# Four of sixteen key pairs get their row maximum through a difference and a ReLU on ScalarE

## The reference

```
h = layernorm(x) * g + b                       # 4096 x 256
q = h @ Wq, k = h @ Wk, v = h @ Wv             # 16 heads of 16 columns each
scores = q k^T / sqrt(16)                      # per head, 4096 queries x 4096 keys
attn = softmax(scores)                         # needs max over the keys of each query
ctx = attn @ v
```

## Time and profile before

| | us |
|---|---|
| median of 3 runs | 3914.32 (3910.07 to 3921.57) |
| the profiled execution's own time | 3921.57 |
| its span in the profile | 3919.8 |

### The profile page before, as it was taken

One profiled execution on the slowest core, in us unless ns is written; L12 is line 12 of the kernel. 1 busy time (PEld: TensorE's weight loads), 2 busy tenths in 40 slices (PEclk: granted clock), 3 DMA queues, 4 the chain that ended last, 5 costly groups with the idle time before them and its releaser, 6 DMA issues. The chain is left out here.

```text
span 3919.8 us, 86423 instructions
## 1 busy us (share of the span) xinstructions
PE 3547.9 (91%) x29108; PEld 1917.4 (49%) x29108; DVE 3020.9 (77%) x5498; ACT 2509.0 (64%) x2773; POOL 697.2 (18%) x703
## 2 busy tenths in 40 slices
PE   7479999999999999999999999999999806999990
PEld 4244444444444444444444444444444605999980
DVE  1638999999999999999999999999996522333335
ACT  2124777777777777777777777777778103555540
POOL 0000000000000000000000000000000357888856
PEclk8686999999999999999999999999999757999995
DMA  2240010110101101010110101011000623444424
GB/s 95 86 143 16 13 20 13 22 20 13 22 11 21 20 12 22 11 21 14 20 21 13 20 13 20 13 22 20 13 13 6 217 89 125 146 137 138 143 83 133
DMA packets 153010, 196.17 MB, mean 50 GB/s; under 512 B 49041, under 2 KB 118545, under 8 KB 148113
## 3 DMA queue, kind: packets, MB, share of 16 engines
q1 hardware_dynamic: 134240, 163.29, 14.9%
q0 software_dynamic: 6336, 16.79, 1.4%
q10 hardware_dynamic: 12144, 12.06, 0.9%
HBM read 128.30 MB, written 62.65 MB: 49 GB/s over the span
## 5 line engine op out<-in xcount | busy, mean ns | idle before, releaser
L725 DVE TENSOR_REDUCE unit_max<-m_ps 128x1 f32<-128x512 f32 x4096 | 2568.3, 684 | 131.4 <-PE m_ps L622 128.7
L704 ACT ACTIVATE probs<-s_ps 128x1024 f32<-128x1024 f32 x2048 | 2084.4, 1026 | 630.0 <-PE s_ps L630 624.6
L645 PE MATMUL o_ps<-probs,v_here 128*32 128x256 f32 (+1 forms) x15360 | 1283.7, 406 | 0.5 <-ACT probs L704 0.5
L622 PE MATMUL m_ps<-k_ring,q_stage 48*128 48x512 f32 x4096 | 1017.8, 422 | 41.5 <-DVE unit_max L725 22.9
L630 PE MATMUL s_ps<-q_stage,k_ring 50*128 50x512 f32 x4096 | 1024.0, 493 | 0.4 <-ACT probs L704 0.4
L630 PEld LDWEIGHTS s_ps<-q_stage,k_ring 50*128 50x128 f32 x4096 | 385.2, 184 | 818.9 <-issue 646.2
L622 PEld LDWEIGHTS m_ps<-k_ring,q_stage 48*128 48x128 f32 x4096 | 665.7, 188 | 183.6 <-DVE unit_max L725 160.3
L645 PEld LDWEIGHTS o_ps<-probs,v_here 128*32 128x32 f32 x15360 | 303.2, 108 | 507.8 <-issue 504.8
L571 POOL TENSOR_TENSOR neg_max<-no_max,tile_max 128x4 f32<-128x4 f32 x127 | 25.3, 199 | 2480.5 <-DVE tile_max L740 2480.5
L1458 DVE TENSOR_TENSOR hidden_low<-h_ps,hidden_high 128x512 fp32r<-128x512 f32 x184 | 127.4, 692 | 366.4 <-ACT hidden_high L1422 366.4
L1418 ACT ACTIVATE h_ps<-h_ps,b_here 128x512 f32<-128x512 f32 x184 | 121.4, 660 | 255.3 <-PE h_ps L1355 255.3
(11 more groups left out here) (175 smaller groups left out, 1948.3 us busy)
## 6 DMA issues: line engine op xcount, KB each, us to landing
w_in<-in_W SPq DMA_DIRECT2D x46, 1024.0 KB, 4.9
q_stage<-max_turned SPq DMA_DIRECT2D x2048, 0.5 KB
q_stage<-qs_dram SPq DMA_DIRECT2D x768, 32.0 KB, 1.8
k_ring<-ks_dram SPq DMA_DIRECT2D x96, 128.0 KB, 4.2
slots_dram<-zero_rows SPq DMA_DIRECT2D x24, 512.0 KB, 6.7
rows_e<-slots_dram SPq DMA_DIRECT2D x24, 512.0 KB, 3.9
y_slots_dram<-y_out ACTq DMA_DIRECT2D x23, 512.0 KB, 4.3
qs_dram<-parts SPq DMA_DIRECT2D x16, 512.0 KB, 2.8
```

The costliest lines, as they stand in the source:

```text
L622: nc.tensor.matmul(m_ps[:, b % 3, :], q_stage[at:at + SROWS, col:col + P], k_ring[at:at + SROWS, par, key:key + CHUNK], start=True, stop=T ...
L645: last = nc.tensor.matmul(o_ps[at:at + SQ, lo:hi], v_here[:, par, first_tile(t) + 2 * k, :], probs[:, t, k, lo:hi], start=(pair == 0), sto ...
L704: nc.scalar.activation(probs[:, t, :, :], s_ps[:, t % 2, :, :], ACT.Exp).then_inc(exp_done, 1)
L725: nc.vector.tensor_reduce(unit_max[:, b, qt, 2 * j + k:2 * j + k + 1], m_ps[:, block_of(t, k) % 3, :], AX.X, ALU.max).then_inc(m_read, 1 + ...
```

## The change

For every query, max(a, b) = b + max(a - b, 0). The change uses this for a pair of key blocks, a from side 0 and b from side 1, in four of the sixteen units of a chunk (`RELU_PAIRS`: 2, 5, 11, 14).

- Key preparation: DVE writes the difference of the two key sides to `k_diff` (a copy of one half out of PSUM, and a subtraction), ACT rounds it to a fifth high part, DVE computes its low part, and SP stores both with two further DMAs per chunk. `low_ready` and `high_ready` count 5 per chunk and not 4.
- SP loads this difference for each head into `kd_ring`, with three further DMAs per head.
- In the four units PE's k = 0 matmul reads `kd_ring` in place of `k_ring`, which gives q(a - b). ACT takes its ReLU out of the bank into `excess` (SBUF), in front of the unit's exponential. DVE adds the other bank to it and takes the maximum, in one `tensor_tensor_reduce`, in place of two reductions.
- The matmul that follows in the first bank's ring place waits for ACT's `excess_ready`, and no longer for `m_read`.

```diff
+RELU_PAIRS = (2, 5, 11, 14)
 ...
             def split(c, b, more):
                 for s in range(4):
-                    dve.wait_ge(high_ready, c * 4 + (s + 1))
+                    if s == 2:
+                        dve.wait_ge(high_ready, c * 5 + 4)
+                        nc.vector.tensor_scalar(k_diff[:, :, :], qk_ps[:, 2:4, HALF:CHUNK], 1.0, None, ALU.mult
+                                                ).then_inc(half_copied, 1)
+                        dve.wait_ge(half_copied, c + 1)
+                        nc.vector.tensor_tensor(k_diff[:, :, :], qk_ps[:, 2:4, 0:HALF], k_diff[:, :, :],
+                                                ALU.subtract).then_inc(diff_ready, 1)
+                    dve.wait_ge(high_ready, c * 5 + (s + 1))
                     nc.vector.scalar_tensor_tensor(parts[:, b, s, 1, :], qk_ps[:, s, :], DH ** -0.5 if s < 2 else 1.0,
                                                    parts[:, b, s, 0, :].bitcast(F32), ALU.mult, ALU.subtract
                                                    ).then_inc(low_ready, 1)
+                dve.wait_ge(high_ready, c * 5 + 5)
+                nc.vector.tensor_tensor(parts[:, b, 4, 1, :].rearrange("p (j t) -> p j t", j=HALVES), k_diff[:, :, :],
+                                        parts[:, b, 4, 0, :].bitcast(F32).rearrange("p (j t) -> p j t", j=HALVES),
+                                        ALU.subtract).then_inc(low_ready, 1)
 ...
                     b = block_of(t, k)
-                    if c * RING_BLOCKS + b > 2:
+                    past = [r for r in RELU_PAIRS if block_of(r, 0) in (b - 3, b - 3 + RING_BLOCKS)]
+                    if past and c * RING_BLOCKS + b > 2:
+                        done = sum(r < t for r in RELU_PAIRS)
+                        pe.wait_ge(excess_ready, it * (PAIR * len(RELU_PAIRS)) + (c * len(RELU_PAIRS) + done))
+                    elif c * RING_BLOCKS + b > 2:
                         pe.wait_ge(m_read, it * (PAIR * RING_BLOCKS) + (c * RING_BLOCKS + b - 2))
+                    ring = kd_ring if k == 0 and t in RELU_PAIRS else k_ring
 ...
+            def excess_pair(n, t):
+                act.wait_ge(m_done, n * (2 * UNITS) + (2 * t + 1))
+                nc.scalar.activation(excess[:, :], m_ps[:, block_of(t, 0) % 3, :], ACT.Relu).then_inc(excess_ready, 1)
 ...
                 for t in range(UNITS):
+                    if ahead and t in RELU_PAIRS:
+                        excess_pair(i + LEAD, t)
                     act.wait_ge(s_done, i * UNITS + (t + 1))
 ...
+                if t in RELU_PAIRS:
+                    dve.wait_ge(excess_ready, n * len(RELU_PAIRS) + (RELU_PAIRS.index(t) + 1))
+                    dve.wait_ge(m_done, n * (2 * UNITS) + (2 * t + 2))
+                    dve.sem_inc(dve_passed, 1)
+                    nc.vector.tensor_tensor_reduce(excess[:, :], m_ps[:, block_of(t, 1) % 3, :], excess[:, :], 1.0, LEAST,
+                                                   ALU.add, ALU.max, unit_max[:, b, qt, 2 * j:2 * j + 1]
+                                                   ).then_inc(m_read, 2 + skip)
+                    return
```

More of the change, by code:

```diff
@@ L52 @@
 LEAST = -3.4e38
-HEAD_DMAS = 16 * 2 * len(K_PARTS)
+HEAD_DMAS = 16 * 3 * len(K_PARTS)
 Q_DMAS = 16 * 2 * len(Q_PARTS)
@@ L133, in linear_attention @@
         hT = sb("hT", [P, 2, HALVES, CHUNK])
-        parts = sb("parts", [P, 2, 4, PARTS, CHUNK], F32R)
+        k_diff = sb("k_diff", [P, HALVES, HALF])
+        parts = sb("parts", [P, 2, 5, PARTS, CHUNK], F32R)
         banks = ps("banks", [P, 8, CHUNK])
@@ L206, in _ @@
                                          ).then_inc(parts_out[b], 16)
-                    sp.wait_ge(parts_out[b], it * 96 + 96)
+                    sp.wait_ge(low_ready, c * 5 + 10)
+                    for j in range(HALVES):
+                        dst = dram["kd"][:, P * j:P * j + P, ds(c * HALF, HALF)]
+                        sp.dma_start(dst.rearrange("n p t -> p n t"),
+                                     parts[:, b, 4, :, HALF * j:HALF * j + HALF].bitcast(F32)).then_inc(parts_out[b], 16)
+                    sp.wait_ge(parts_out[b], it * 128 + 128)
                     sp.sem_inc(parts_free, 1)
             for b in range(2):
-                sp.wait_ge(parts_out[b], 16 * 6 * CHUNKS // 2)
+                sp.wait_ge(parts_out[b], 16 * 8 * CHUNKS // 2)
             sp.wait_ge(x1_out, 16)
@@ L341, in split @@
                                          scale=(DH ** -0.5 if s < 2 else 1.0)).then_inc(high_ready, 1)
+                act.wait_ge(diff_ready, c + 1)
+                nc.scalar.activation(parts[:, b, 4, 0, :], k_diff[:, :, :], ACT.Copy).then_inc(high_ready, 1)
                 if more:
@@ L487, in load_head @@
                                      dram["ks"][part, ds(h * DH, DH), side, :]).then_inc(head_in, 16)
+                for n, part in enumerate(K_PARTS):
+                    sp.dma_start(kd_ring[DH * n:DH * n + DH, ds(par, 1), :].bitcast(F32).rearrange("r a k -> r (a k)"),
+                                 dram["kd"][part, ds(h * DH, DH), :]).then_inc(head_in, 16)
             def load_q(h, qc, buf):
@@ L619, in max_pair @@
                     b = block_of(t, k)
-                    if c * RING_BLOCKS + b > 2:
+                    past = [r for r in RELU_PAIRS if block_of(r, 0) in (b - 3, b - 3 + RING_BLOCKS)]
[3 more added lines that the diff above has]
+                    elif c * RING_BLOCKS + b > 2:
                         pe.wait_ge(m_read, it * (PAIR * RING_BLOCKS) + (c * RING_BLOCKS + b - 2))
+                    ring = kd_ring if k == 0 and t in RELU_PAIRS else k_ring
                     nc.tensor.matmul(m_ps[:, b % 3, :], q_stage[at:at + SROWS, col:col + P],
-                                     k_ring[at:at + SROWS, par, key:key + CHUNK], start=True, stop=True).then_inc(m_done, 1)
+                                     ring[at:at + SROWS, par, key:key + CHUNK], start=True, stop=True).then_inc(m_done, 1)
             def scores(it, c, t):
@@ L697, in copy_o, with chunk @@
                 nc.scalar.activation(o_here[:, :], o_ps[:, :], ACT.Copy).then_inc(o_copied, 1)
-            def chunk(i, first=False):
+            def chunk(i, ahead, first=False):
                 for t in range(UNITS):
+                    if ahead and t in RELU_PAIRS:
+                        excess_pair(i + LEAD, t)
                     act.wait_ge(s_done, i * UNITS + (t + 1))
@@ L706, in chunk @@
                         copy_o(i)
-            chunk(0, first=True)
-            with act.Fori(1, RING) as i:
-                chunk(i)
+            for n in range(LEAD):
+                for t in RELU_PAIRS:
+                    excess_pair(n, t)
+            chunk(0, True, first=True)
+            with act.Fori(1, RING - LEAD) as i:
+                chunk(i, True)
+            for i in range(RING - LEAD, RING):
+                chunk(i, False)
             copy_o(RING)
```

18 lines of the change are left out of this document (11 added, 7 removed).

## The result

The changed kernel takes 4078.47 us (median of 4, 4068.58 to 4079.67), against 3916.47 before (median of 4): a ratio of 1.041, 95% interval 1.0386 to 1.0432. It is slower, by 162 us, where 87 were forecast. The profiled execution's span is 4078.9 us, 159.1 more than before.

What follows compares the result with a forecast made beforehand. PE and a ring of latencies over three banks were taken to bound the attention. 66 (attention) + 17.5 (key preparation) + 2.6 + 1.9 - 1 = 87 us on 3921.6 gave 4009, median 4002; range 3925 to 4090.

Steps and rivals of the forecast that it cites:

- The ring of latencies: Attention: three banks' time from filled to free gives 1.60 us per unit, beside 1.57 for PE alone.
- four late places: Attention, units 2, 5, 11, 14: VectorE free 0.17 later delays PE two units on; 0.53 us per chunk net, 66 in all.
- The sum's length: ReLU units on VectorE: 0.60 us for the sum plus 0.07 for the column write behind it, bounds nothing and 0.235.
- The handoff: ReLU units, from ScalarE's ReLU to VectorE's sum: 0.03 us plus 0.08 for the second wait.
- The key preparation: Key stage: VectorE's added copy, subtraction and low part make each of seven chunks 2.50 us longer, 17.5 in all.
- The stage's end: End of key preparation: the last two stores follow the last low part and delay the next stage by 2.6 us.
- the further loads ahead of the attention: Ahead of the first head: nothing hides SP's three further loads of 0.63 us each, 1.9 us in all.
- The eight ReLU pairs ahead of the first scores: Before the first scores: they save VectorE work but wait for the ReLU; between 0 and -4 us, taken as -1.
- The exponential stays hidden: ReLU units on ScalarE: the exponential moves behind the ReLU, ends at 2.28, needed by PE at 2.48 or later.
- VectorE's throughput as the bound: Attention, rival: four pairs give VectorE 2.1 us back per chunk, making the kernel 62 us faster, 3852 us; chance 8%.
- The sum at half pace: ReLU units, rival: the sum takes 1.20 us and not 0.60, 298 us more, kernel at 4300; chance 7%.
- VectorE's busy share: Attention, sign in the profile after: VectorE's busy share falls to some 87%.

Runs made afterwards that it cites:

- The first and second bank shortened in turn: Kernel before, VectorE's reduction of each unit's first, then second, bank over 256 of 512 columns: 3806.91 and 3862.61 us, against 3907.48.
- the swapped waits: Changed kernel, VectorE's two waits in front of the sum in the other order, the ReLU's on the sum itself: 4011.5 us, ratio 1.0243.
- the half ReLU: Changed kernel with VectorE's two waits in the other order, and ScalarE's ReLU over 256 of 512 columns: 3943.15 us, against 3907.48 before.
- the single places: Changed kernel with a ReLU pair in unit 5 alone, then in unit 11 alone: 3973.59 and 3981.93 us, chunk 21.38 and 21.45 us.
- one wait: Changed kernel with the next chunk's normalization moved earlier, ReLU waiting for both matmuls and the sum for the ReLU only: 3998.34 us, ratio 1.0216.
- the further loads alone: Changed kernel's attention and three further loads per head, with the key preparation of before and no further store: 4048.54 us, ratio 1.0344.

## Why the prediction was right in sign and half in size

The forecast was +87 us with a range of 3925 to 4090, and 4078.47 lies inside it, near its top. The sign and the mechanism were right; that the range held is in part luck. Its upper end came from the column write at 0.235 us in each of four places (+148), which turned out to cost next to nothing. What cost more was the handoff, for which the bounds held nothing above the 0.11 of the sum.

- *The ring of latencies bounds the attention, together with PE's own work*: right. The first and second bank shortened in turn, the swapped waits, the half ReLU and the single places each show it.
- *First bank free earlier, second later; four late places; nothing for the saved reductions*: the places were right. Units 4, 7, 12 and 0 are the long ones, as forecast, by 0.27, 0.28, 0.28 and 0.20, where the sum had 0.11 to 0.16 net for each. The small gain from the first bank (0.02 a place) was not tested by itself.
- *The sum's length, 0.60 + 0.07*: 0.62, so 0.05 too much. The column write is hidden in all but 0.01 or 0.02.
- *The handoff, 0.03 + 0.08 = 0.11*: the term that was mis-sized. It measured 0.27, 0.16 more, and the two parts of it were wrong by different amounts. The way from ScalarE to a sum with one wait was taken as 0.03 from the key preparation, and is 0.14 (waits swapped, and one wait). The second wait was taken as 0.08 from ScalarE's exponential, and is 0.13 together with the semaphore step that stands between it and the sum; no run separates these two. Nor does a run show why the first is 0.14: in the changed kernel's own preparation the handoff from ScalarE to VectorE is still 0.03 (242.38 to 242.41), so it is not the pair of engines alone. Four times (0.16 - 0.05) is 0.44, and 0.53 + 0.44 = 0.97 of the 0.98 measured; the 0.44 are 54 us. With 0.14 as the handoff, the sum gives 21.17 + 0.53 + 4 x (0.03 - 0.05) = 21.62, and the swapped waits gave 21.63.
- *The key preparation, +2.50 per chunk*: the work was right (3.15 against 3.14), but PE's idle of 3.5 us cost its clock behind five of seven chunks. Seven chunks are 26.7 us longer where the term had 17.5: 9 us that no term had.
- *The stage's end, 2.6, and the further loads ahead of the attention, 1.9*: the right places, too small: 4.4 and 2.7. The first counted two stores behind the difference's low part where six queue up. For the second, the issue of three loads explains half (1.4); the rest is there with the further loads alone (3.1 in all), and no run shows what it is.
- *The eight ReLU pairs ahead of the first scores, -1*: 0.0.
- *The exponential stays hidden*: right. PE's waits for exponentials at values are 0.5 us in both kernels. At the scores' weight loads the profile names the exponential more often (182 times from 1000 to 2000, before 95), but such a load follows the one before it by 0.41 where it waits for nothing as well. Swapping VectorE's waits gave back 0.52 of the chunk and leaves the exponential where it is; the half ReLU moves it by 0.2 too, and so does not settle this alone.
- *VectorE's throughput as the bound*, the rival on the other side: refuted, above all by the half reductions. *The sum at half pace*: refuted by 692 ns.
- *VectorE's busy share, "some 87%"*, one of the signs: 80% (402.1 of 500). The forecast share did not follow from its own terms: VectorE's 20.3 us of a chunk less the 2.1 saved are 84% of 21.7, and the chunk became longer than that.

The column write was also priced, as an estimate of 0.165 us, from the some 158 cycles of the Trainium skill ("VectorE: DVE Perf Modes", section "Side-by-side: where the cycles go for N=2048 bf16"). That was further off than my 0.07: it lasts 84 ns and delays its follower by less than 0.02.

## What to carry to other kernels

Before work is moved off an engine that is 96% busy, look at what the busy engine holds: here three banks in a ring, whose time from filled to free was, beside PE's own work, the bound, so that an engine in between made it longer while it took work away. When an instruction waits for two signals, put the one that comes last on the instruction itself; the order of two lines was worth 67 us. A wait added to a stage that PE shares can cost its clock as well as the wait. Take the price of a handoff from the instruction that will receive it, or give it a bound of its own: 0.03 us read at another instruction was 0.14 here.

## What the runs showed of the hardware

- From a ReLU's end to a `tensor_tensor_reduce` on VectorE: 0.14 us with the wait on the sum itself, 0.27 with the wait in front of a semaphore step and a second wait. From a ScalarE copy's end to a `tensor_scalar` on VectorE, in the key preparation: 0.03.
- A `tensor_tensor_reduce` of 128x512 from PSUM and SBUF lasts 692 ns, and the next instruction starts 0.62 behind its start, the accumulator read (84 ns) included; a plain reduction's follower starts 0.60 behind it.
- PE idle of 3.50 us in a stage at 2.4 GHz: behind five of seven such stretches the granted clock fell, to 0.50 in the row from 249 to 250, and eight value matmuls took up to 3.51 us against 1.89; behind two it stayed at 1.00. With idle stretches of 0.98 us, in the kernel before, it stayed up.
